# Sums of squares of the second attention's queries: four accumulating squares on ScalarE in place of one square and a VectorE reduction

## The chip, the cores and the metric

The kernel runs on one core of one Trainium2 chip. Its time is the device time of one execution in microseconds (us). A core has TensorE (PE in the rows: matrix products and transposes), VectorE (DVE), ScalarE (ACT), GpSimd (POOL) and SyncE (SP, which here issues DMAs). Each engine works through its own list of instructions in order, and they wait for one another by semaphores.

## What is computed

A transformer block in fp32 on 16 sequences of 128 tokens with 256 features: a first attention with adaptive layer norm (16 heads of 128), a GELU network, a second attention with 16 query heads and 4 key/value heads, and a mixture of 8 experts of which each token uses 2. The change lies in the second attention, where queries and keys are normalised head by head before the rotation:

```python
h = rmsnorm(hidden, attn_norm_w)
q = (h @ q_w.T).reshape(B, S, Hq, hd)        # Hq = 16, hd = 128
k = (h @ k_w.T).reshape(B, S, Hkv, hd)       # Hkv = 4
v = (h @ v_w.T).reshape(B, S, Hkv, hd)
q = rmsnorm(q, q_norm_w).transpose(0, 2, 1, 3)   # x * rsqrt(mean(x*x) + eps) * w
k = rmsnorm(k, k_norm_w).transpose(0, 2, 1, 3)
q = apply_rope(q, cos, sin)
k = apply_rope(k, cos, sin)
scores = jnp.einsum('bhqd,bhkd->bhqk', q, k) * scale   # causal, then softmax
attn = jnp.einsum('bhqk,bhkd->bhqd', jax.nn.softmax(scores, axis=-1), v)
hidden = hidden + attn @ o_w.T
```

The norm of a query head is a single factor for each token and head, so the kernel does not apply it to the query but to the scores: it is the scale of the exponential.

## The kernel before

Everything is written out in Bass: a list of instructions for each engine, with hand-placed semaphores. The products are made in three parts (high by high, high by low, low by high part of fp32 numbers split into two), so most results in PSUM are copied twice: ScalarE writes the high part, VectorE subtracts it and writes the low part.

The second attention runs from about 650 to 1100 us of the span. It is a software pipeline over 64 **units**: 16 sequences by 4 key/value heads (`kv`), a unit being the 4 query heads of one key/value head for the 128 tokens of one sequence, a tile of 128 x 512. `NG` = 4 groups of `GB` = 4 sequences, so 16 steps (`s.u` = 0 to 15) a group. `step(s)` on each engine does one stage for several units at once, and there are 7 more steps at the end in which no new unit is begun. In the step in which unit n is begun:

- **TensorE**: in the first step of each sequence the key projection into bank 1 and the value projection into bank 2; the query projection of unit n into bank 0 (L1958, 12 products with the split parts); the output product of unit n-6 (L2015); the product of weights and values of unit n-5 into bank 6 (L2042); transposes of the queries of unit n-1 into bank 4 (L2074) and of the weights of unit n-4 into bank 5 (L2082); mask and scores of unit n-2 into bank 3 (L2104, L2107). The next query projection waits for `g_qb` (rotation done) and `g_sq` (square done), since both read bank 0. The scores wait for `g_ex`, the exponentials of unit n-3 out of the same bank 3.
- **ScalarE**: the exponentials of unit n-3 (L891), four instructions of 128 x 128 with the scale `rq`, the bias `nb` and an accumulator that leaves the row sums in `rsum`; at a new sequence the square of the keys (L900); the square `sq` of the queries of unit n (L905, 128 x 512, out of bank 0); then the copies `o2_hi` (L912), `q_t` (L917), `pt_hi` (L924), and `v_hi` or `k_t` in the first or second step of a sequence.
- **VectorE**: the row maximum `nmax` of unit n-3 (L1552) and `nb` = `nmax` times `rq` (L1556); the rotation of keys (new sequence) and of queries out of banks 1 and 0, two instructions each (L1510, L1514); the reciprocal `rinv` of the row sums (L1578); the sum of squares of the keys; the sum of squares of the queries `q_ms` (L1589, a reduction of 128 x 512 to 128 x 4); then `o2_lo` (L1593), the residual `xres` once a sequence (L1598), `pt_lo` (L1601), `v_lo` once a sequence. Parts of norm, routing and weight splitting stand behind that, before the next step's `nmax`.
- **GpSimd**: adds the two parts of the rotation (L644), multiplies the weights by `rinv` (L648), and makes `rq` from `q_ms`: adds eps (L656), then the power -1/2 (L660). `rq` of unit n is used three steps later, by `nb` and by the exponentials. Once a sequence it does the same for the keys (`rk`).

`bank[6][:]` and the like are banks of PSUM, 512 fp32 numbers a partition each. The tile `p2` is called `p` in the rows of the trace and `p_123` in the lists of instructions; `o2_hi` and `o2_lo` are `o_hi` and `o_lo` there. The first attention (to about 560 us) and the experts (from about 1100 us) are not touched.

Of the kernel before, what the change touches and what calls it, by code (L numbers as in the profile page):

```python
# [23 lines left out]
ALU = mybir.AluOpType  # L24
ACT = mybir.ActivationFunctionType
X = mybir.AxisListType.X
# [4 lines left out]
GB = 4  # L31
NG = B // GB
GT = GB * T
H, DH = 16, 128
HKV = 4
REP = H // HKV
# [12 lines left out]
SCALE = DH ** -0.5  # L49
# [4 lines left out]
def program(nc, ins, out):  # L54
    ctx = ExitStack()
    with ctx:
# [15 lines left out]
        def sem(name):  # L72
            return ctx.enter_context(nc.semaphore(name))
# [75 lines left out]
        sq = sb("sq", [P, REP * DH], at=W2 + 6 * KB)  # L149
        kr = sb("kr", [P, HKV * DH], at=W2 + 8 * KB)  # L150
        kb = sb("kb", [P, HKV * DH], at=W2 + 10 * KB)
# [16 lines left out]
        q_ms = sb("q_ms", [P, 2, REP], at=small)  # L168
# [5 lines left out]
        nb = sb("nb", [P, 2, REP], at=small + 224)  # L174
# [63 lines left out]
        bank = [ctx.enter_context(nc.psum_tensor(f"bank{i}", [P, 512], F32)) for i in range(8)]  # L238
# [27 lines left out]
        def lo1(c, i):  # L266
# [24 lines left out]
            sem(f"g_{x}") for x in ("kp", "vp", "qp", "tp", "qtp", "op", "pvp", "ktp", "sp"))  # L291
        g_ex, g_ksq, g_sq, g_ph, g_vh, g_qt, g_oh, g_kt = (
            sem(f"g_{x}") for x in ("ex", "ksq", "sq", "ph", "vh", "qt", "oh", "kt"))
        g_x, g_mx, g_nb, g_kb, g_qb, g_ks, g_kr, g_pl, g_ss, g_ri, g_vl, g_ol = (
            sem(f"g_{x}") for x in ("x", "mx", "nb", "kb", "qb", "ks", "kr", "pl", "ss", "ri", "vl", "ol"))
        g_ka, g_rk, g_kv, g_qr, g_rq, g_qv, g_pn = (
            sem(f"g_{x}") for x in ("ka", "rk", "kv", "qr", "rq", "qv", "pn"))

# [87 lines left out]
        def _(sp):  # L386
# [73 lines left out]
            def load_tile(i):  # L460

                if i == 0:
                    sp.wait_ge(g_qr, NG * 4 * GB)
                    sp.wait_ge(g_ss, NG * 4 * GB)
                    sp.wait_ge(g_ktp, B)
                    sp.wait_ge(s_v, S_LIST)
                    sp.wait_ge(d_send[0], 16 * 2 * BC[0])
                if i == TC[0]:
                    sp.wait_ge(d_send[1], 16 * 2 * BC[1])
                if i >= NX:  # L470
                    sp.wait_ge(e_xp, i - NX + 1)
                    sp.wait_ge(s_goal, i - NX + 1)
                if i < TC[0]:
                    at = sp.value_load(base_i[0:1, i:i + 1], min_val=0, max_val=ROWS[0] - P)
                    sp.dma_start(xs[:, i % NX], xs_dram[0][bass.ds(at, P)]).then_inc(d_ring[i % NX], 16)
                else:
                    at = (i - TC[0]) * P
                    sp.dma_start(xs[:, i % NX], xs_dram[1][at:at + P]).then_inc(d_ring[i % NX], 16)
# [26 lines left out]
            for i in range(NX - 1):  # L505
                load_tile(i)
# [21 lines left out]
        def _(pool):  # L528
# [108 lines left out]
            def step(s):  # L637
                n, new_seq = s.n, s.new() and s.kv == 0
# [11 lines left out]
                                            ALU.mult).then_inc(g_pn, 1)  # L650
                if s.new():

                    pool.wait_ge(g_ss, n + 1)
                    if s.had(2):
                        pool.wait_ge(g_rq, n - 1)
                    nc.gpsimd.tensor_tensor(q_ve[:, s.u % 2], q_ms[:, s.u % 2], eps[:, 0:REP], ALU.add).then_inc(g_qv, 1)  # L656
                    pool.wait_ge(g_qv, n + 1)
                    if s.had(4):
                        pool.wait_ge(g_ex, n - 3)
                    nc.gpsimd.tensor_tensor(rq[:, s.u % 4], q_ve[:, s.u % 2], neg_half[:, 0:REP], ALU.pow).then_inc(g_rq, 1)  # L660
# [58 lines left out]
        def _(act):  # L719
# [105 lines left out]
            n = NG * H  # L825
# [47 lines left out]
            def step(s):  # L873
                n, new_seq = s.n, s.new() and s.kv == 0
# [10 lines left out]
                if s.live(3):  # L885
# [4 lines left out]
                    for j in range(REP):  # L890
                        last = nc.scalar.activation(p2[:, (s.u - 3) % 2, j], bank[3][:, j * T:(j + 1) * T], ACT.Exp,  # L891
                                                    scale=rq[:, (s.u - 3) % 4, j:j + 1],
                                                    bias=nb[:, (s.u - 3) % 2, j:j + 1],
                                                    accum_out=rsum[:, (s.u - 3) % 2, j:j + 1])
# [5 lines left out]
                    nc.scalar.activation(ksq[:], bank[1][:], ACT.Square, scale=SCALE).then_inc(g_ksq, 1)  # L900
                if s.new():
                    act.wait_ge(g_qb, n + 1)
                    if s.had(1):
                        act.wait_ge(g_ss, n)
                    nc.scalar.activation(sq[:], bank[0][:], ACT.Square, scale=SCALE).then_inc(g_sq, 1)  # L905
                if s.u == 12 and not s.first:
                    router_exp(s.g - 1)
                if s.live(5):
# [71 lines left out]
            def expert(i):  # L980
# [6 lines left out]
                if 0 <= i - 3 < NT:  # L987
                    expert_out(i - 3)

            attention2(step, expert)  # L990
            for i in range(len(DRAIN), NT + 3):
                expert(i)
# [7 lines left out]
        def _(dve):  # L1000
# [424 lines left out]
            n = NG * H  # L1425
# [93 lines left out]
            def step(s):  # L1519
                n, new_seq, prev = s.n, s.new() and s.kv == 0, 3 * NG + s.g - 1  # L1520
# [60 lines left out]
                if new_seq:  # L1581
                    dve.wait_ge(g_ksq, s.seq + 1)
                    nc.vector.tensor_reduce(k_ms[:], ksq[:].rearrange("p (h d) -> p h d", d=DH), X,
                                            ALU.add).then_inc(g_ks, 1)
                if s.new():
                    dve.wait_ge(g_sq, n + 1)
                    if s.had(2):
                        dve.wait_ge(g_rq, n - 1)
                    nc.vector.tensor_reduce(q_ms[:, s.u % 2], sq[:].rearrange("p (h d) -> p h d", d=DH), X,  # L1589
                                            ALU.add).then_inc(g_ss, 1)  # L1590
                if s.live(5):
                    dve.wait_ge(g_oh, n - 4)
                    nc.vector.tensor_tensor(o2_lo[:], bank[6][:], o2_hi[:].bitcast(F32), ALU.subtract).then_inc(g_ol, 1)  # L1593
# [674 lines left out]
```

## Time and profile before

| what | us |
|---|---|
| median of 3 runs | 1257.84 |
| lowest and highest of them | 1256.36, 1258.54 |
| the profiled execution | 1245.22 |
| its span (first to last instruction) | 1243.5 |
| VectorE busy | 793.6 (64%) |
| ScalarE busy | 655.5 (53%) |
| TensorE (matmul) busy | 1154.7 (93%) |
| GpSimd busy | 520.4 (42%) |

The profile is of one execution, which was 12.6 us shorter than the median of the runs. In the rows below, a time at the start of a row is the start of an instruction from the start of the span, and the bracket at its end is the idle time of that engine before it with what ended it. "PEld" is the weight load of TensorE, which overlaps its products.

### The profile page before, as it was taken

The page shows a single profiled execution, that of the slowest core. Times are in us where ns is not written, and L with a number is a line of the kernel's source. Part 1 is how long each engine was busy: PE and PEld are TensorE (multiplying, and loading weights), DVE is VectorE, ACT ScalarE, POOL GpSimd, SP SyncE. Part 2 cuts the span into 40 slices and gives each one's busy share as a digit, 9 for nine tenths or more (in the row PEclk, how much of TensorE's full clock was granted, in tenths as well). Part 3 has the DMA queues.
Part 4 walks back from the last instruction along what each step waited for, and adds up shares of the span by engine and source line. Part 5 has one row for each costly group of instructions (what it writes and reads, how often), then busy time and mean ns, then how long its engine had stood idle before and what let it go on. Part 6 is the DMA issues. An engine that isn't in the chain of part 4 may idle for free.

```text
span 1243.5 us, 23075 instructions
## 1 busy us (share of the span) xinstructions
PE 1154.7 (93%) x7776; PEld 1040.7 (84%) x7808; DVE 793.6 (64%) x1699; ACT 655.5 (53%) x1866; POOL 520.4 (42%) x597
## 2 busy tenths in 40 slices
PE   6999999999999999989988999998999999758995
PEld 5888999999999999978876888987887898657895
DVE  3666554345434553367557888888787888757666
ACT  3445444444444444465545766656756665545553
POOL 4111131113111311143347656665875786633753
PEclk9999999999999999999999999999999999989998
DMA  9100000000000011041001029400000100223546
GB/s 339 59 1 1 18 1 18 1 1 1 18 1 1 1 38 48 1 186 35 18 18 52 1 78 302 125 2 1 23 14 1 56 23 5 47 71 106 172 130 199
DMA packets 46454, 68.81 MB, mean 55 GB/s; under 512 B 4741, under 2 KB 38537, under 8 KB 45355
## 3 DMA queue, kind: packets, MB, share of 16 engines
q1 hardware_dynamic: 42595, 58.89, 15.2%
q0 software_dynamic: 3744, 8.43, 1.9%
q8 instruction: 66, 1.08, 0.4%
q14 instruction: 49, 0.40, 0.1%
HBM read 41.17 MB, written 27.97 MB: 56 GB/s over the span
## 4 chain that ended last, share of the span: by engine, by line
PE 67%; DVE 9%; ACT 6%; issue 4%; POOL 3%; DMA 2%; SPq 0%; ACTq 0%; DVEq 0%; POOLq 0%
PE bank L1770 12%; PE bank L1807 9%; PE bank L1958 7%; PE bank L1838 6%; PE bank L2015 5%; PE bank L1798 4%; PE bank L1780 4%; PE bank L2148 4%; PE bank L2107 3%; PE bank L2179 2%; ACT p L891 2%; PE bank L2042 2%; PE bank L1899 2%; PE bank L1788 2%; PE bank L2074 1%
## 5 line engine op out<-in xcount | busy, mean ns | idle before, releaser
L570 POOL TENSOR_TENSOR p<-p,rinv 128x512 f32<-128x512 f32 x64 | 66.5, 1040 | 409.3 <-DVE rinv L1340 409.3
L891 ACT ACTIVATE p<-bank,nb,rq 128x128 f32<-128x128 f32 x256 | 113.9, 454 | 133.4 <-DVE nb L1556 133.3
L760 ACT ACTIVATE p<-bank,nmax 128x128 f32<-128x128 f32 x256 | 90.7, 367 | 117.1 <-DVE nmax L1328 117.1
L644 POOL TENSOR_TENSOR qr<-qr,rb 128x512 f32<-128x512 f32 x64 | 81.6, 1276 | 95.7 <-DVE rb L1514 95.1
L1336 DVE COPY pt<-bank 128x512 f32<-128x512 f32 x64 | 44.2, 691 | 107.2 <-PE bank L1788 104.4
L1770 PE MATMUL bank<-cur_hi,wqk_hi 128*128 128x512 f32 x256 | 108.6, 424 | 4.1 <-DVE cur_lo L1281 4.1
L1770 PE MATMUL bank<-cur_hi,wqk_lo 128*128 128x512 f32 x256 | 101.5, 397 | 0.0
L1770 PE MATMUL bank<-cur_lo,wqk_hi 128*128 128x512 f32 x256 | 101.4, 396 | 0.0
L769 ACT ACTIVATE o_hi<-bank,bqkv 128x512 fp32r<-128x512 f32 x64 | 44.2, 691 | 100.3 <-PE bank L1798 100.0
L1344 DVE SCALAR_TENSOR_TENSOR o_lo<-bank,bqkv,o_hi 128x512 fp32r<-128x512 f32 x64 | 48.0, 751 | 52.8 <-ACT o_hi L769 52.8
L2107 PE MATMUL bank<-k_t,q_t 128*128 128x128 f32 x512 | 68.3, 277 | 12.3 <-ACT p L891 10.5
L1807 PE MATMUL bank<-wo_hi,o_hi 128*128 128x256 f32 x256 | 77.5, 303 | 0.6 <-DVE o_lo L1344 0.4
L2015 PE MATMUL bank<-wo_hi,o_hi 128*128 128x256 f32 x256 | 74.1, 289 | 4.2 <-DVE o_lo L1593 4.2
L1798 PEld LDWEIGHTS bank<-pt,v 128*128 128x128 f32 x512 | 66.3, 191 | 13.0 <-DVE pt L1336 8.5
L1838 PE MATMUL bank<-wv_hi,cur_hi 128*128 128x256 f32 x256 | 76.7, 300 | 0.0
L1798 PE MATMUL bank<-pt,v 128*128 128x128 f32 x512 | 67.9, 275 | 6.2 <-DVE pt L1336 6.2
L2015 PE MATMUL bank<-wo_hi,o_lo 128*128 128x256 f32 x256 | 72.9, 285 | 0.0
L2015 PE MATMUL bank<-wo_lo,o_hi 128*128 128x256 f32 x256 | 72.8, 285 | 0.0
L1807 PE MATMUL bank<-wo_hi,o_lo 128*128 128x256 f32 x256 | 72.2, 282 | 0.0
L1807 PE MATMUL bank<-wo_lo,o_hi 128*128 128x256 f32 x256 | 72.0, 281 | 0.0
L1838 PE MATMUL bank<-wv_lo,cur_hi 128*128 128x256 f32 x256 | 71.3, 278 | 0.0
L1838 PE MATMUL bank<-wv_hi,cur_lo 128*128 128x256 f32 x256 | 71.1, 278 | 0.0
(271 smaller groups left out, 3880.5 us busy)
## 6 DMA issues: line engine op xcount, KB each, us to landing
token_scratch<-empty SPq DMA_DIRECT2D x1, 13287.0 KB, 47.3
xs<-token_scratch SPq DMA_DIRECT2D x46, 129.0 KB, 2.2
wqk_raw<-in_wqk SPq DMA_DIRECT2D x8, 512.0 KB, 10.6
gate<-gates_scratch SPq DMA_DIRECT2D x8, 512.0 KB, 3.9
got_t<-expert_scratch SPq DMA_DIRECT2D x16, 256.0 KB, 3.7
w_raw<-in_w SPq DMA_DIRECT2D x2, 1408.0 KB, 6.3
xres<-in_x SPq DMA_DIRECT2D x4, 512.0 KB, 9.5
wv_raw<-in_wv SPq DMA_DIRECT2D x8, 256.0 KB, 10.5
```

What stands on the lines that cost most here:

```text
L570: nc.gpsimd.tensor_tensor(p1[:, h % 2], p1[:, h % 2], rinv[:, h % 2].unsqueeze(2).broadcast_to([P, GB, T]), ALU.mult).then_inc(a_pn, 1)
L644: nc.gpsimd.tensor_tensor(qr[:, s.u % 2], qr[:, s.u % 2], rb[:], ALU.add).then_inc(g_qr, 1)
L760: last = nc.scalar.activation(p1[:, h % 2, b], bank[3][:, b * T:(b + 1) * T], ACT.Exp, bias=nmax[:, h % 2, b:b + 1], accum_out=rsum[:, h % ...
L891: last = nc.scalar.activation(p2[:, (s.u - 3) % 2, j], bank[3][:, j * T:(j + 1) * T], ACT.Exp, scale=rq[:, (s.u - 3) % 4, j:j + 1], bias=n ...
L1770: last = pe.matmul(dst, l, r, start=(k == 0 and i == 0), stop=(k == KD - 1 and i == 2))
L1780: last = pe.matmul(bank[3][:, bs], q1[:, h % 2, bs], k1[:, h % 2, bs], start=True, stop=True)
L1798: last = pe.matmul(bank[5][:, bs], v1[:, h // 2 % 2, b, h % 2 * DH:h % 2 * DH + DH], pt1[:, bs], start=True, stop=True)
L1807: last = pe.matmul(bank[banks[b // 2]][:, b % 2 * D:b % 2 * D + D], l, r, start=(first and b % 2 == 0 and i == 0), stop=(last_one and i == 2),
L1838: last = pe.matmul(bank[2][:, j * 2 * DH:(j + 1) * 2 * DH], l, r, start=(k == 0 and i == 0), stop=(k == KD - 1 and i == 2))
L1958: last = pe.matmul(dst, l, r, start=(k == 0 and i == 0), stop=(k == KD - 1 and i == 2))
L2015: last = pe.matmul(bank[7][:, 0:D], l, r, start=(kv == 0 and j == 0 and i == 0), stop=(kv == HKV - 1 and j == REP - 1 and i == 2))
L2107: last = pe.matmul(bank[3][:, js], q_t[:, s.u % 2, js], k_t[:, slot, kv * T:(kv + 1) * T], start=False, stop=(j == REP - 1), skip_group_ch ...
```

## The change

ScalarE squares the queries in four instructions of 128 x 128, one for each head, and each leaves the sum of its row in `q_ms` by its accumulator. VectorE's reduction, its waits and its semaphore `g_ss` are gone; whoever waited for `g_ss` (GpSimd's L656, and SyncE once at the start of the experts) waits for `g_sq`. ScalarE no longer waits for the reduction of the unit before; it waits instead for `rq` of the unit two before, since it now writes `q_ms`. The squares themselves are still written to `sq`, which nobody reads.

```diff
@@ SyncE, before the first expert tile
-                    sp.wait_ge(g_ss, NG * 4 * GB)
+                    sp.wait_ge(g_sq, NG * 4 * GB)
@@ GpSimd, step
-                    pool.wait_ge(g_ss, n + 1)
+                    pool.wait_ge(g_sq, n + 1)
@@ ScalarE, step
                     act.wait_ge(g_qb, n + 1)
-                    if s.had(1):
-                        act.wait_ge(g_ss, n)
-                    nc.scalar.activation(sq[:], bank[0][:], ACT.Square, scale=SCALE).then_inc(g_sq, 1)
+                    if s.had(2):
+                        act.wait_ge(g_rq, n - 1)
+                    for j in range(REP):
+                        last = nc.scalar.activation(sq[:, j * DH:(j + 1) * DH], bank[0][:, j * DH:(j + 1) * DH], ACT.Square,
+                                                    scale=SCALE, accum_out=q_ms[:, s.u % 2, j:j + 1])
+                    last.then_inc(g_sq, 1)
@@ VectorE, step
-                if s.new():
-                    dve.wait_ge(g_sq, n + 1)
-                    if s.had(2):
-                        dve.wait_ge(g_rq, n - 1)
-                    nc.vector.tensor_reduce(q_ms[:, s.u % 2], sq[:].rearrange("p (h d) -> p h d", d=DH), X,
-                                            ALU.add).then_inc(g_ss, 1)
```

ScalarE in a plain step of the second group, with the semaphores that each instruction waits for. Before:

```order
L891 ACTIVATE p_123,rsum<-bank,nb,rq 128x128 [waits g_tp,g_nb]
L891 ACTIVATE p_123,rsum<-bank,nb,rq 128x128 x3
L905 ACTIVATE sq<-bank 128x512 [waits g_ss,g_qb]
L912 ACTIVATE o_hi<-bank 128x512 [waits g_op,g_pvp]
L917 ACTIVATE q_t<-bank 128x512 [waits g_sp,g_qtp]
L924 ACTIVATE pt_hi<-bank 128x512 [waits g_pvp,g_tp]
```

ScalarE at the same place, now:

```order
L891 ACTIVATE p_123,rsum<-bank,nb,rq 128x128 [waits g_tp,g_nb]
L891 ACTIVATE p_123,rsum<-bank,nb,rq 128x128 x3
L906 ACTIVATE sq,q_ms<-bank 128x128 [waits g_rq,g_qb]
L906 ACTIVATE sq,q_ms<-bank 128x128 x3
L915 ACTIVATE o_hi<-bank 128x512 [waits g_op,g_pvp]
L920 ACTIVATE q_t<-bank 128x512 [waits g_sp,g_qtp]
L927 ACTIVATE pt_hi<-bank 128x512 [waits g_pvp,g_tp]
```

The square has become four instructions at the same place, ahead of all three copies. The read-out that follows each accumulating instruction is not listed here; the trace shows it as ACTIVATION_READ_ACCUMULATOR.

## Rows read from the trace of the kernel before

**Rows 1.** The page, busy time of each engine, share of span, instructions:

```profile
PE 1154.7 (93%) x7776; PEld 1040.7 (84%) x7808; DVE 793.6 (64%) x1699; ACT 655.5 (53%) x1866; POOL 520.4 (42%) x597
```

**Rows 2.** Stretches: start:end, length, busy us per engine, granted clock, DMA:

```profile
774.17:799.44 25.27, 25.17 (x168) 22.77 (x169) 21.25 (x47) 17.03 (x51) 15.93 (x20) 1.00 0.65 184
700.00:1070.00 370.00, 355.25 (x2330) 314.77 (x2357) 305.30 (x647) 240.88 (x714) 251.74 (x306) 1.00 0.18 53
```

**Rows 3.** Waits from 700 to 1070 us: total us, times, longest:

```profile
ACT p L891 <- DVE nb L1556: 109.4, 54, 3.1
...
DVE pt_lo L1601 <- ACT pt_hi L924: 14.4, 41, 1.6
...
DVE q_ms L1589 <- ACT sq L905: 14.1, 41, 0.6
ACT o_hi L912 <- PE bank L2042: 7.0, 6, 1.2
...
ACT q_t L917 <- PE bank L2074: 4.4, 4, 1.2
...
DVE kr L1510 <- PE bank L1958: 2.7, 3, 0.9
```

**Rows 4.** Timeline of ScalarE in a plain step: start, duration, instruction:

```profile
789.91 0.46 ACT L891 ACTIVATE p<-bank,nb,rq 128x128 f32<-128x128 f32 x1 [1.19 <-DVE nb L1556]
...
791.24 0.46 ACT L891 ACTIVATE p<-bank,nb,rq 128x128 f32<-128x128 f32 x1
...
791.67 0.60 ACT L905 ACTIVATE sq<-bank 128x512 f32<-128x512 f32 x1
792.15 0.61 ACT L912 ACTIVATE o_hi<-bank 128x512 fp32r<-128x512 f32 x1
792.63 0.62 ACT L917 ACTIVATE q_t<-bank 128x512 f32<-128x512 f32 x1
793.11 0.63 ACT L924 ACTIVATE pt_hi<-bank 128x512 fp32r<-128x512 f32 x1
795.36 0.46 ACT L891 ACTIVATE p<-bank,nb,rq 128x128 f32<-128x128 f32 x1 [1.62 <-DVE nb L1556]
```

**Rows 5.** Timeline of VectorE in the same step:

```profile
792.31 0.69 DVE L1589 TENSOR_REDUCE q_ms<-sq 128x4 f32<-128x512 f32 x1 [0.31 <-ACT sq L905]
...
793.77 0.69 DVE L1601 TENSOR_TENSOR pt_lo<-bank,pt_hi 128x512 fp32r<-128x512 f32 x1 [0.18 <-ACT pt_hi L924]
794.37 0.68 DVE L1552 TENSOR_REDUCE nmax<-bank 128x4 f32<-128x512 f32 x1
795.16 0.16 DVE L1556 TENSOR_TENSOR nb<-nmax,rq 128x4 f32<-128x4 f32 x1
```

**Rows 6.** ScalarE in the first attention: two starts, then groups by form:

```profile
300.34 0.36 ACT L760 ACTIVATE p<-bank,nmax 128x128 f32<-128x128 f32 x1
...
300.68 0.37 ACT L760 ACTIVATE p<-bank,nmax 128x128 f32<-128x128 f32 x1
...
L760 ACT ACTIVATION_READ_ACCUMULATOR p<-bank,nmax 128x1 f32 x6 | 1.2, 200 | 0.0
...
L785 ACT ACTIVATE q<-bank,bqkv 128x512 f32<-128x512 f32 x1 | 0.7, 687 | 0.2 <-PE bank L1770 0.2
```

**Rows 7.** Timeline, second group: where ScalarE and VectorE waited for TensorE:

```profile
780.54 0.60 ACT L912 ACTIVATE o_hi<-bank 128x512 fp32r<-128x512 f32 x1 [1.24 <-PE bank L2042]
...
805.80 0.60 ACT L912 ACTIVATE o_hi<-bank 128x512 fp32r<-128x512 f32 x1 [1.09 <-PE bank L2042]
...
834.87 0.60 ACT L917 ACTIVATE q_t<-bank 128x512 f32<-128x512 f32 x1 [1.23 <-PE bank L2074]
...
860.51 0.69 DVE L1510 TENSOR_TENSOR kr<-bank,rope 128x512 f32<-128x512 f32 x1 [0.86 <-PE bank L1958]
```

**Rows 8.** Timeline, ScalarE's last read-out, then TensorE's scores after it:

```profile
772.49 0.21 ACT L891 ACTIVATION_READ_ACCUMULATOR p<-bank,nb,rq 128x1 f32 x1
...
772.90 0.38 PE L2104 MATMUL bank<-mask,ident_b 128*128 128x512 bf16 x1
...
848.55 1.05 PE L2107 MATMUL bank<-k_t,q_t 128*128 128x128 f32 x8 [1.36 <-ACT p L891]
```

More of the change, by code:

```diff
@@ L293, in program @@
             sem(f"g_{x}") for x in ("ex", "ksq", "sq", "ph", "vh", "qt", "oh", "kt"))
-        g_x, g_mx, g_nb, g_kb, g_qb, g_ks, g_kr, g_pl, g_ss, g_ri, g_vl, g_ol = (
-            sem(f"g_{x}") for x in ("x", "mx", "nb", "kb", "qb", "ks", "kr", "pl", "ss", "ri", "vl", "ol"))
+        g_x, g_mx, g_nb, g_kb, g_qb, g_ks, g_kr, g_pl, g_ri, g_vl, g_ol = (
+            sem(f"g_{x}") for x in ("x", "mx", "nb", "kb", "qb", "ks", "kr", "pl", "ri", "vl", "ol"))
         g_ka, g_rk, g_kv, g_qr, g_rq, g_qv, g_pn = (
```

## The prediction

> **What bounds the kernel now.** I read the page's busy times first, then the stretches, the waits and the timelines of the second attention, since the change touches nothing else. TensorE is busy for 93% of the span [rows 1] and for 355 of the 370 us from 700 to 1070 us [rows 2]; in a quiet sequence (774.17 to 799.44, four steps) it is busy for 25.17 of 25.27 us. That looks like a stretch bound by TensorE, behind which ScalarE (241 us busy of 370) could hide anything. The waits say that there is more to it. ScalarE waits for `nb` in all 54 steps, 109.4 us in all, about 2 us a step [rows 3], and this is no free time: it is the other half of a loop that runs through ScalarE and VectorE in every step. In a plain step the loop can be read off start by start [rows 4, 5]: first exponential 789.91 to square 791.67 (1.76), to `o_hi` 792.15 (0.48), to `q_t` 792.63 (0.48), to `pt_hi` 793.11 (0.48), to VectorE's `pt_lo` 793.77, which waited for `pt_hi` (0.66), to `nmax` 794.37 (0.60), to `nb` 795.16 (0.79), to the next exponential 795.36 (0.20). The sum is 5.45 us, which is the whole step. `nmax` stands behind `pt_lo` on VectorE, and the exponentials stand ahead of the copies on ScalarE, so no part of this loop can slip past another. TensorE's work for a plain step is as long, and in the first step of a sequence longer by the key and value projections. So two bounds lie side by side: TensorE is the later one at one or two points of each sequence, the loop in the steps between.
>
> How much room the loop has is what it waits for TensorE: `o_hi` 7.0 us in 6 waits, `q_t` 4.4 us in 4, `kr` 2.7 us in 3, together 14.1 us [rows 3]. In the second group these are 1.24 and 1.09 (`o_hi`, steps 4 and 8), 1.23 (`q_t`, step 12) and 0.86 (`kr`, step 0 of the next group) [rows 7].
>
> **What the change removes.** 64 reductions on VectorE, 0.69 us each and 0.60 from start to start [rows 5], 38 us. None of it is on the loop: in the plain step `pt_lo` still had to wait 0.18 us for `pt_hi` after reduction and `o_lo` were over [rows 5], and in 41 of 54 steps it did so, 14.4 us in all [rows 3]. Without the reduction `o_lo` can't begin earlier than `o_hi` ends, and `o_hi` now stands behind four squares. I cost the removal at 0. What hides it is ScalarE's chain of copies; were that chain shorter by more than 0.2 us a step, the reduction would be worth something.
>
> **What it adds.** On ScalarE one square, 0.48 us from its start to the start of `o_hi` [rows 4], becomes four of 128 x 128, each with a read-out of the accumulator. No row shows a square in this form. The nearest are the exponentials of the same shape with read-out: with scale and bias from memory 0.44 from start to start (789.91 to 791.24 is three of them, 1.33 us [rows 4]), with the bias alone from memory 0.34 (300.34 to 300.68 [rows 6]). Each operand from memory so costs about 0.09 us. The square has neither: at 128 x 512 it takes 0.60 [rows 4], while the copy with one such operand takes 0.687 [rows 6], the same 0.09. So I take 0.44 - 2 x 0.09 = 0.26 us for each square with its read-out, 1.04 for four, in place of 0.48: **d = 0.56 us a step**. The bounds: 0.20 each, if only the read-out itself (200 ns [rows 6]) is the limit, d = 0.32; 0.34 each, if an accumulating square costs what the cheaper exponential does, d = 0.90; 0.44 each, d = 1.28. The nearest is the middle of the first two, since both differences of 0.09 point there.
>
> The Trainium skill, page "ScalarE: Activation LUTs", section "What ACT_TABLE_LOAD costs", gives 186 ns plus 0.833 ns an element for an ACTIVATE with immediate operands, about 93 ns for each operand by pointer, and an overlap of about 93 ns between neighbours. The 0.09 of the rows agrees with its 93 ns; for the new square it gives 293 ns, and with a read-out of 200 ns and two overlaps 0.31 a square, d = 0.76, by which the steps below would come to +35 us.
>
> **Where d goes.** Squares stand beside exponentials in 61 of the 64 steps (the first three units come before the first exponential). If nothing took it up, the loop would be 61 x 0.56 = 34 us longer. I go from one wait on TensorE to the next; there the loop's delay is taken up as far as TensorE was late, but TensorE itself has meanwhile been pushed by the exponentials, behind which its scores stand. In the second group:
> - Steps 1 to 4, to the `o_hi` that waited 1.24. TensorE's scores follow ScalarE's last read-out at 772.49 + 0.21 within 0.2 us, and all after it ran without a break [rows 8]. It is pushed by the squares of steps 0, 1 and 2, 3d less under 0.1, 1.6 us; the loop by 5d - 1.24 = 1.6. The later counts: +1.6.
> - Steps 5 to 8, `o_hi` waited 1.09: 4d - 1.09 = +1.15. TensorE arrived later than the exponentials here and is pushed less.
> - Steps 9 to 12, `q_t` waited 1.23: 4d - 1.23 = +1.0.
> - Steps 13 to 16. The routing on VectorE makes the loop longer and TensorE waits for it, 1.36 us at once at 848.55 [rows 8]. So it is pushed in full by three squares: 3d - 0.15 = +1.5; the fourth is taken up by the 0.86 of `kr`.
>
> That is 5.3 us for the second group and as much for the third; in the last nothing takes up the fourth square, 5.4. The first group has no wait for TensorE but a `q_t` of 0.7 (4.4 less three of 1.23 [rows 3]) and the next group's `kr` (0.9): 15 x 0.56 less 0.7 and 0.7 = 7.0. Sum 23 us, less about 1 for waits too short for the list: **+22 us**. After the last square the pipeline drains into the experts as before, and carries the delay to the end.
>
> **Other edits.** GpSimd waits for `g_sq` in place of `g_ss`. The last read-out ends about 3 x 0.26 + 0.4 = 1.15 us after the first square's start; the reduction ended at 792.31 + 0.69 = 793.00, 1.33 after 791.67. `rq` comes 0.2 us earlier, and is used three steps later: 0. TensorE's next query projection waits for `g_sq`, which now comes 0.5 us later; in a plain step it is still in its scores by then, cost 0 to 0.3 us once a group. The new wait of ScalarE for `rq` of two units before has been met a step ago; queued behind it are the squares and all copies, but it costs 0. SyncE's wait falls after the last unit, 0.
>
> **Rivals.**
> - *Hidden.* TensorE, at 96% in this stretch, sets the pace and ScalarE's 2 us a step of idle time take the 0.56. For it speaks that in the quiet sequence TensorE never waits; against it, that the loop fills the plain step to the last 0.01. It would give 0 to +2 us, 1258.
> - *Dear read-outs.* The square costs 0.34 with its read-out. By the same steps with d = 0.90: 12.1 for the first group, then 10.7, 10.7 and 10.8, +44 us, 1302. At 0.44 it is +68.
> - *VectorE relieved, faster.* In 13 of 54 steps `pt_lo` did not wait for `pt_hi` [rows 3]; there VectorE may be the late one, and the loop would run `sq`, `q_ms`, `o_lo`, `pt_lo`. Without `q_ms` 13 x 0.6 = 8 us come off, 1250. It decides from d under 0.2, where the four squares end no later than reduction and `o_lo` let the loop go; the bound of 0.20 a square already gives d = 0.32.
> - *Nothing taken up*, +34 us, 1292: the waits on TensorE go along with the loop. I count it to the upper half of the forecast.
>
> **How the numbers follow.** The profiled execution took 1245.2 us, with a span of 1243.5; it is 12.6 under the median of the runs, 1257.8, and I put the 22 us on the median: 1280. Chances: forecast and its margins (+6 to +36) 0.71, dear read-outs (+36 to +70) 0.11, hidden or almost (within 2.5 us, 0.2%, about what a measurement of this kernel can tell) 0.10, a small loss of 2.5 to 6 us 0.02, faster 0.06. So slower 0.84, same 0.10, faster 0.06. The range, 1264 to 1302, runs from d = 0.32 (by the same steps +0.9, +0.2, +0.1 and +0.8 in a group, some 10 us with the first, and a little below) to d = 0.90, and leaves out the hidden case, the gain and the dearest read-outs, 0.2.
>
> **What would show it.** In the profile after: squares 0.28 us long, 0.26 from start to start; a plain step of 6.0 us from exponential to exponential; waits of `o_hi` and `q_t` for TensorE nearly gone; TensorE idle before the scores (waiting for exponentials) in most steps, up by some 20 us; `pt_lo` waiting about 0.7 us for `pt_hi` in each step; VectorE busy 38 us less, ScalarE some 36 us more. The forecast is wrong if the squares start 0.34 or more apart, or if the plain step stays at 5.45 us.

## The result, and the profile after

The changed kernel takes **1282.03 us** (median of 4 runs, 1277.19 to 1283.62), the kernel before beside it 1257.87 (1256.36 to 1258.54). That is 24.2 us more, a ratio of **1.0193, 95% interval 1.0164 to 1.0221**. The forecast was 1280, range 1264 to 1302, slower with a chance of 0.84.

The profiled execution of after took 1281.76 us, with a span of 1280.0, 36.5 more than the span of before. Only some 26 of these belong to the change, as the windows show (start:end, length, busy us of TensorE, weight load, VectorE, ScalarE and GpSimd, then granted clock, DMA). First after, from the first exponential to the last and from there to the end:

```profile
667.10:1123.10 456.00, 413.20 (x2622) 360.71 (x2652) 319.09 (x695) 310.96 (x1252) 293.14 (x346) 0.98 0.16 48
1123.10:1280.00 156.90, 126.89 (x811) 113.97 (x810) 93.03 (x278) 71.20 (x204) 70.28 (x66) 0.89 0.43 131
```

Before, the same two stretches:

```profile
664.50:1096.70 432.20, 401.77 (x2626) 355.44 (x2656) 354.73 (x756) 278.12 (x825) 291.92 (x347) 1.00 0.17 50
1096.70:1243.50 146.80, 118.09 (x809) 106.80 (x807) 96.38 (x278) 70.58 (x204) 70.14 (x66) 0.92 0.46 140
```

The pipeline grew by 23.8 us and began 2.6 later. The experts' part behind it, which the change doesn't touch, was 10.1 longer, with a granted clock of 0.89 where it was 0.92. In a second profile of the same kernel (e5 below) it lasted 146.9 us, as before, and between 144.7 and 148.5 in those of e1, e2, e3, e6, e7, e8 and e9. So these 10 us are no effect of the change.

The busy times answer [rows 1]. VectorE has 42 us less, ScalarE 35 more:

```profile
PE 1177.2 (92%) x7776; PEld 1055.7 (82%) x7808; DVE 751.2 (59%) x1635; ACT 690.8 (54%) x2314; POOL 524.0 (41%) x597
```

The squares and their read-outs, all of them: least, median and greatest duration in ns, first and last start.

```profile
L906 ACT ACTIVATE sq<-bank x256: 268/281/308, 652.8 to 1101.3; 128x128 f32<-128x128 f32 x128
L906 ACT ACTIVATION_READ_ACCUMULATOR sq<-bank x256: 194/215/243, 652.9 to 1101.5; 128x1 f32 x128
```

ScalarE in a plain step, against [rows 4]. Line numbers are 3 higher than before from the squares' code down to the removed reduction, and 3 lower behind it; the names are the same:

```profile
800.90 0.46 ACT L891 ACTIVATE p<-bank,nb,rq 128x128 f32<-128x128 f32 x1 [1.14 <-DVE nb L1559]
...
802.66 0.28 ACT L906 ACTIVATE sq<-bank 128x128 f32<-128x128 f32 x1
802.82 0.21 ACT L906 ACTIVATION_READ_ACCUMULATOR sq<-bank 128x1 f32 x1
802.91 0.29 ACT L906 ACTIVATE sq<-bank 128x128 f32<-128x128 f32 x1
...
803.66 0.64 ACT L915 ACTIVATE o_hi<-bank 128x512 fp32r<-128x512 f32 x1
804.14 0.64 ACT L920 ACTIVATE q_t<-bank 128x512 f32<-128x512 f32 x1
804.62 0.65 ACT L927 ACTIVATE pt_hi<-bank 128x512 fp32r<-128x512 f32 x1
806.89 0.46 ACT L891 ACTIVATE p<-bank,nb,rq 128x128 f32<-128x128 f32 x1 [1.62 <-DVE nb L1559]
```

VectorE in the same step, against [rows 5]:

```profile
804.33 0.69 DVE L1590 TENSOR_TENSOR o_lo<-bank,o_hi 128x512 fp32r<-128x512 f32 x1 [1.34 <-ACT o_hi L915]
805.30 0.69 DVE L1598 TENSOR_TENSOR pt_lo<-bank,pt_hi 128x512 fp32r<-128x512 f32 x1 [0.28 <-ACT pt_hi L927]
805.91 0.68 DVE L1555 TENSOR_REDUCE nmax<-bank 128x4 f32<-128x512 f32 x1
806.69 0.16 DVE L1559 TENSOR_TENSOR nb<-nmax,rq 128x4 f32<-128x4 f32 x1
```

The loop, start by start: exponential to square 1.76, four squares to `o_hi` 1.00 (one square had 0.48), `q_t` 0.48, `pt_hi` 0.48, `pt_lo` 0.68, `nmax` 0.61, `nb` 0.78, next exponential 0.20. The sum is 5.99 us against 5.45, and all but 0.02 of the difference is the squares. VectorE has no reduction any more, and stands idle for 1.34 us until `o_hi` comes.

The waits from 700 to 1100 us, against [rows 3] (total us, times, longest):

```profile
ACT p L891 <- DVE nb L1559: 114.1, 56, 3.4
...
DVE o_lo L1590 <- ACT o_hi L915: 72.5, 55, 1.6
...
DVE pt_lo L1598 <- ACT pt_hi L927: 17.1, 42, 1.4
...
PE bank L2104 <- ACT p L891: 12.9, 11, 2.3
PE bank L2101 <- ACT p L891: 9.0, 13, 2.1
...
ACT q_t L920 <- PE bank L2071: 3.5, 4, 1.0
...
PE bank L1955 <- ACT sq L906: 0.2, 1, 0.2
```

The idle time that VectorE won turned into a new wait of its own, for `o_hi`, 72.5 us in 55 steps. The wait of `o_hi` for TensorE, 7.0 us in [rows 3], is gone; that of `q_t` is only down from 4.4 to 3.5. TensorE's query projection (L1955) waited for the squares only once here, 0.2 us.

Where the delay builds up, read from the start of an exponential at each boundary (us; "e5" is the second profile of the same kernel):

| exponential | before | after | e5 | added, after | added, e5 | forecast |
|---|---|---|---|---|---|---|
| the first | 664.46 | 667.10 | 666.28 | 2.6 | 1.8 | 0 |
| second group | 751.21 | 760.83 | 758.67 | 7.0 | 5.6 | 7.0 |
| third group | 859.70 | 874.22 | 871.93 | 4.9 | 4.8 | 5.3 |
| fourth group | 968.96 | 989.05 | 988.12 | 5.6 | 6.9 | 5.3 |
| the last | 1096.72 | 1123.10 | 1123.38 | 6.3 | 7.5 | 5.4 |

Each row gives what was added since the row above it. Step by step, from first exponential to first exponential, 10 of the 16 steps of the second group (counted from 0) grew by 0.49 to 0.55 us, step 0 by 0.42 and step 9 by 0.67. Step 1 stayed as it was. Steps 4, 8 and 12, in which `o_hi` or `q_t` had waited for TensorE, became shorter by 0.62, 0.65 and 0.24. So the squares cost their 0.52 in steps of every length, not in the plain ones alone, and are taken up above all where TensorE had been late.

### The profile page after: what moved, and what is told of

It reads as the page before. It is cut to its first block, busy times and chain, and to the rows that moved or that the text cites. A ratio compares the mean times of both kernels' runs of the same rounds, so it can differ in the third digit from the quotient of the medians.

```text
span 1280.0 us, 23396 instructions
## 1 busy us (share of the span) xinstructions
PE 1177.2 (92%) x7776; PEld 1055.7 (82%) x7808; DVE 751.2 (59%) x1635; ACT 690.8 (54%) x2314; POOL 524.0 (41%) x597
## 3 DMA queue, kind: packets, MB, share of 16 engines
q1 hardware_dynamic: 42595, 58.89, 14.6%
## 4 chain that ended last, share of the span: by engine, by line
PE 53%; DVE 13%; ACT 12%; issue 6%; POOL 5%; DMA 2%; another core or an unknown queue 0%; SPq 0%; ACTq 0%; DVEq 0%; POOLq 0%
PE bank L1767 11%; PE bank L1804 9%; PE bank L1835 6%; ACT p L891 4%; PE bank L1795 4%; PE bank L2145 4%; PE bank L1955 4%; PE bank L1777 4%; ACT sq L906 3%; PE bank L2176 2%; DVE nmax L1555 2%; DVE pt_lo L1598 2%; PE bank L1785 2%; PE bank L1896 2%; PE bank L2012 2%
## 5 line engine op out<-in xcount | busy, mean ns | idle before, releaser
L1590 DVE TENSOR_TENSOR o_lo<-bank,o_hi 128x512 fp32r<-128x512 f32 x64 | 44.3, 692 | 82.5 <-ACT o_hi L915 82.5
L2104 PE MATMUL bank<-k_t,q_t 128*128 128x128 f32 x512 | 69.7, 280 | 17.2 <-ACT p L891 16.2
L906 ACT ACTIVATE sq<-bank 128x128 f32<-128x128 f32 x256 | 67.5, 284 | 15.7 <-DVE rb L1517 14.8
```

The costliest lines, as they stand in the source:

```text
L906: last = nc.scalar.activation(sq[:, j * DH:(j + 1) * DH], bank[0][:, j * DH:(j + 1) * DH], ACT.Square, scale=SCALE, accum_out=q_ms[:, s.u ...
L2104: last = pe.matmul(bank[3][:, js], q_t[:, s.u % 2, js], k_t[:, slot, kv * T:(kv + 1) * T], start=False, stop=(j == REP - 1), skip_group_ch ...
```

## The experiments

My theory is the prediction's: a loop through ScalarE and VectorE binds the plain steps, the squares lie on it and the reduction didn't, and TensorE's lateness in the first step of a sequence takes a little back. The rivals are that something else carries the cost (TensorE's projection behind `g_sq`, the read-outs alone) and that the reduction was worth something after all. Differences in us are of medians, ratios come from the paired comparison; the two can differ by up to 1.7 us. The chips of these runs were some 11 us faster for both kernels than that of the first result: the kernel before took 1246.4 in the runs of e1 to e4, 1246.6 in those of e5 to e8, and 1244.6 in those of e9 to e11. The whole times in the expectations of e1 to e4 were worked out from the first result, so only their differences can be held against what was measured.

**e5, the changed kernel again**, unedited, for its difference on these chips.

> The changed kernel again, beside the others of this call. +22 to +26 us against the kernel before on the same chip, whatever that chip's level is; the pipeline of the second attention longer by 24 to 27 us, the experts and the first attention the same but for TensorE's granted clock.

Measured: 1271.1, +24.5 us, ratio 1.0205 [1.0181, 1.0229]; plain step 5.98. The level of the chip doesn't change the difference. Against this number the others are read.

**e2, the reduction away and the square left whole.** GpSimd adds eps to the first four squares of the tile, in place of the sums, so the normalisation of the queries is left out.

```diff
-                    nc.gpsimd.tensor_tensor(q_ve[:, s.u % 2], q_ms[:, s.u % 2], eps[:, 0:REP], ALU.add).then_inc(g_qv, 1)
+                    nc.gpsimd.tensor_tensor(q_ve[:, s.u % 2], sq[:, 0:REP], eps[:, 0:REP], ALU.add).then_inc(g_qv, 1)
...
-                    for j in range(REP):
...
+                    if s.had(1):
+                        act.wait_ge(g_qv, n)
+                    nc.scalar.activation(sq[:], bank[0][:], ACT.Square, scale=SCALE).then_inc(g_sq, 1)
```

> Only the removal: one square of 128x512 as before and no reduction on VectorE; GpSimd makes rq from four of the squares (so the query norm is not the reference's). The loop theory: the reduction was beside the loop, 0 to -3 us against the kernel before (1255 to 1258). Rival, that VectorE was the late one in the steps where pt_lo did not wait: -8 us or more, below 1250.

Measured: 1246.77 against 1246.4, ratio 0.9993 [0.9980, 1.0006]; plain step 5.44. The removal by itself, 64 reductions and 38 us of VectorE's time, is worth nothing. The rival by which a relieved VectorE gains 8 us falls.

**e7, the split alone**: in the kernel before, four plain squares without an accumulator, reduction kept.

```diff
-                    nc.scalar.activation(sq[:], bank[0][:], ACT.Square, scale=SCALE).then_inc(g_sq, 1)
+                    for j in range(REP):
+                        last = nc.scalar.activation(sq[:, j * DH:(j + 1) * DH], bank[0][:, j * DH:(j + 1) * DH], ACT.Square,
+                                                    scale=SCALE)
+                    last.then_inc(g_sq, 1)
```

> The kernel before with four squares of 128x128 without accumulator, and the reduction kept. Start to start 0.28 - 0.12 = 0.16 us, four of them 0.65 in place of 0.48: d = 0.17. Between two reads of the waits on TensorE: +2 to +6 us. Rival, the number of ScalarE instructions is what costs, not the read-out: above +12.

Measured: 1253.04, +6.5 us, ratio 1.006 [1.0038, 1.0081], plain step 5.63. Timeline of ScalarE in e7; the four squares stand in one row:

```profile
790.48 0.79 ACT L906 ACTIVATE sq<-bank 128x128 f32<-128x128 f32 x4
791.13 0.63 ACT L915 ACTIVATE o_hi<-bank 128x512 fp32r<-128x512 f32 x1
```

Four squares take 0.65 us to the start of `o_hi`, 0.16 each, in place of 0.48. With its read-out each takes 0.25. So of the 0.52 us a step 0.17 is the split and 0.35 the four read-outs, and of the 24.5 us about 6.5 and 18, the split counted first. In this profile TensorE's granted clock fell to half twice (862 to 866 and 975 to 978 us), so part of the 6.5 us may be the clock's; the plain step isn't touched by it.

**e3, two squares of 128 x 256 with accumulator.** Two sums a row stand in for four, so the queries of two heads share one.

```diff
-                    for j in range(REP):
-                        last = nc.scalar.activation(sq[:, j * DH:(j + 1) * DH], bank[0][:, j * DH:(j + 1) * DH], ACT.Square,
+                    for j in range(2):
+                        last = nc.scalar.activation(sq[:, j * 256:(j + 1) * 256], bank[0][:, j * 256:(j + 1) * 256], ACT.Square,
```

> The changed kernel with two accumulating squares of 128x256 in place of four of 128x128 (each sum is over two heads, so the norm is not the reference's). Start to start 0.25 + 128 x 0.83 ns = 0.36 us, two of them 0.71 in place of 0.48: d = 0.23 us a step. With the waits on TensorE taking up delay as predicted: 2.1 in the first group, then about 1.2 each, +6 us (1263). Rival, each microsecond on ScalarE counts in proportion (24 us for 0.55): +10 us (1268). Rival, the read-out as such is dear: above 1270.

Measured: 1254.79, +8.4 us, ratio 1.0062 [1.0040, 1.0084], plain step 5.69. Timeline of ScalarE in e3:

```profile
801.11 0.38 ACT L908 ACTIVATE sq<-bank 128x256 f32<-128x256 f32 x1 [0.76 <-DVE rb L1519]
...
801.49 0.38 ACT L908 ACTIVATE sq<-bank 128x256 f32<-128x256 f32 x1
...
801.84 0.60 ACT L917 ACTIVATE o_hi<-bank 128x512 fp32r<-128x512 f32 x1
```

Two squares take 0.73, +0.25 a step, half of what four add, for about a third of the time.

**e6, eight squares of 128 x 64**, the odd ones with their sums into a spare tile; each of the four sums that are used is then over half a head.

```diff
-                    for j in range(REP):
-                        last = nc.scalar.activation(sq[:, j * DH:(j + 1) * DH], bank[0][:, j * DH:(j + 1) * DH], ACT.Square,
-                                                    scale=SCALE, accum_out=q_ms[:, s.u % 2, j:j + 1])
+                    for j in range(2 * REP):
+                        last = nc.scalar.activation(sq[:, j * 64:(j + 1) * 64], bank[0][:, j * 64:(j + 1) * 64], ACT.Square,
+                                                    scale=SCALE, accum_out=(q_ms, q_hx)[j % 2][:, s.u % 2, j // 2:j // 2 + 1])
```

> The changed kernel with eight accumulating squares of 128x64 (each sum is over half a head, so the norm is not the reference's). Start to start 0.25 - 64 x 0.83 ns = 0.20 us, eight of them 1.58 in place of 0.48: d = 1.1 us a step. Now the waits on TensorE are used up: by the steps of the prediction 15 in the first group, then 14 each, +57 us. Rival, in proportion to the 24 us of d = 0.55: +48. Rival, ScalarE's idle 2 us a step still take it (TensorE or the clock set the time): within 35.

Measured: 1305.69, +59.1 us, ratio 1.0481 [1.0457, 1.0505]; plain step 6.60. Timeline of ScalarE in e6, the first two squares and `o_hi`:

```profile
821.83 0.22 ACT L907 ACTIVATE sq<-bank 128x64 f32<-128x64 f32 x1 [0.77 <-DVE rb L1518]
...
822.04 0.22 ACT L907 ACTIVATE sq<-bank 128x64 f32<-128x64 f32 x1
...
823.42 0.65 ACT L916 ACTIVATE o_hi<-bank 128x512 fp32r<-128x512 f32 x1
```

Eight squares take 1.59 us, d = 1.11. Added squares pass on to the end almost whole once the waits that can take them up are used up: 0.59 more a step made 34.6 us more, where 61 steps of it are 36. TensorE's query projection now waited for the squares too, 17.5 us in 33 waits over the whole stage (3.4 in 5 in the changed kernel), but the plain step is still the loop: 5.99 with the squares' 1.00 replaced by 1.59 is 6.58.

Together, d = 0, 0.17, 0.25, 0.52 and 1.11 gave 0, +6.5, +8.4, +24.5 and +59.1 us. This is no straight line through zero: of the first quarter of a microsecond about half is hidden, of the rest little.

**e1, the changed kernel with `pt_hi` ahead of `q_t`.** It takes one copy of 0.48 us off the loop and leaves ScalarE's work the same.

```diff
-                if s.live(1):
-                    act.wait_ge(g_qtp, n)
...
                 (pt_hi)
+                if s.live(1):
+                    act.wait_ge(g_qtp, n)
...
```

> The changed kernel, with ScalarE's copies q_t and pt_hi in the other order in each step (pt_hi first). The loop theory (exponentials, squares, o_hi, q_t, pt_hi, then VectorE's pt_lo and nmax, set the step): q_t leaves the loop, 0.48 us a step, so the plain step falls from 6.0 us to TensorE's 5.5, and the kernel loses nearly all of the 24 us: 1260, between 1256 and 1266. Rival, that TensorE is held by the later end of the squares (it reads bank 0 only after them) or by anything else than this loop: no change, 1278 to 1284, plain step 6.0 us.

Measured: 1261.48, +15.1 us against the kernel before, ratio 1.0109 [1.0092, 1.0125]. 9.4 of the 24.5 us came back, not nearly all. Timeline of VectorE in e1, a plain step:

```profile
804.40 0.69 DVE L1590 TENSOR_TENSOR o_lo<-bank,o_hi 128x512 fp32r<-128x512 f32 x1 [1.34 <-ACT o_hi L915]
805.00 0.68 DVE L1598 TENSOR_TENSOR pt_lo<-bank,pt_hi 128x512 fp32r<-128x512 f32 x1
805.60 0.68 DVE L1555 TENSOR_REDUCE nmax<-bank 128x4 f32<-128x512 f32 x1
```

`pt_lo` no longer waits for anything: it stands behind `o_lo`, which begins 0.67 us after `o_hi` and takes 0.60. The loop now runs squares, `o_hi`, `o_lo`, `pt_lo`; it is 5.60 us long and not 5.5, still 0.15 over the kernel before. That the loop binds is shown, since an exchange of two copies of equal work is worth 9 us. The squares lie on both of its branches. The measured 1261.48 lies in the expected 1256 to 1266 only because this chip is faster; by the difference, +15 where about +2 was expected, the expectation failed. The rival, no change at all, falls as well. 61 steps of 0.15 are 9 of the 15.1 us; the rest lies in the first units and in the steps that are not plain, and I didn't take it apart.

**e4, the same exchange in the kernel before** (the diff is that of e1, with its square whole and its reduction kept).

> The kernel before with the same swap as e1, pt_hi ahead of q_t. Loop theory: the loop is 0.48 us shorter in each step, but TensorE's 5.5 us bound the plain step already, so only the steps in which TensorE waited for exponentials gain: -4 to -12 us (1246 to 1254). Rival, TensorE or VectorE alone bounds it: no change.

Measured: 1246.79 against 1246.4, ratio 0.9999 [0.9981, 1.0018]. The plain steps did become shorter, 5.45 to 5.17, with VectorE's reduction now on the loop (timeline of VectorE in e4: three instructions without a gap, the first after the square):

```profile
819.12 0.69 DVE L1589 TENSOR_REDUCE q_ms<-sq 128x4 f32<-128x512 f32 x1 [0.31 <-ACT sq L905]
819.72 0.68 DVE L1593 TENSOR_TENSOR o_lo<-bank,o_hi 128x512 fp32r<-128x512 f32 x1
820.32 0.68 DVE L1601 TENSOR_TENSOR pt_lo<-bank,pt_hi 128x512 fp32r<-128x512 f32 x1
```

But the first step of a sequence gave it all back: 8.48 us in place of 7.91 (801.09 to 809.57), with `o_hi` waiting for TensorE, then `pt_hi` too. Timeline of ScalarE there:

```profile
805.49 0.60 ACT L912 ACTIVATE o_hi<-bank 128x512 fp32r<-128x512 f32 x1 [1.37 <-PE bank L2042]
806.37 0.60 ACT L919 ACTIVATE pt_hi<-bank 128x512 fp32r<-128x512 f32 x1 [0.28 <-PE bank L2082]
```

**e11, e2 with the exchange**: no reduction and the shorter loop. The normalisation is left out as in e2, and its edit is those of e2 and e1 together.

> e4 (pt_hi ahead of q_t) and e2 (one square, no reduction; the query norm is not the reference's) together. In e4 the reduction is on the loop, so ScalarE and VectorE now need less than 5.17 us a plain step. If TensorE's work is the other bound throughout, as e4 says, nothing comes of it: -3 to +2 us against before. If the loop still held the kernel, -5 to -10.

Measured: 1242.72 against 1244.56, ratio 0.9991 [0.9971, 1.0011], plain step 5.07. Even 0.38 us less loop in each plain step is worth nothing measurable. Before, TensorE was the other bound, as close behind as the prediction had it: 25.17 of 25.27 us in a quiet sequence [rows 2]. The loop can be made longer at a price and not shorter at a gain.

**e8 and e9, the new form for the first unit of a sequence alone, and for the other three alone.** The rest keeps the whole square and the reduction.

```diff
+        ACC = (0,)
...
+                    if s.kv in ACC:
...
+                        for j in range(REP):
+                            last = nc.scalar.activation(sq[:, j * DH:(j + 1) * DH], bank[0][:, j * DH:(j + 1) * DH],
+                                                        ACT.Square, scale=SCALE, accum_out=q_ms[:, s.u % 2, j:j + 1])
+                        last.then_inc(g_sq, 1)
+                    else:
+                        nc.scalar.activation(sq[:], bank[0][:], ACT.Square, scale=SCALE).then_inc(g_sq, 1)
...
-                if s.new():
+                if s.new() and s.kv not in ACC:
```

In e9 it is `ACC = (1, 2, 3)`.

> The change in the first step of each sequence only (16 of 64 units; one square and the reduction in the other 48). If the waits on TensorE take up delay where they stand, d is taken up there whole: steps 4, 8 and 12 of a group cost nothing, step 0 some 0.5, together 0 to +3 us against before. Rival, each of the 64 costs its share of 24 us: +6 us.

> The complement of e8: the change in the second, third and fourth step of each sequence (48 of 64 units), one square and the reduction in the first. If the waits on TensorE in the first steps take up delay: the 24.5 us less the 2.1 of e8, and less again because three delays of 0.53 meet a wait of 1.1 to 1.2 instead of four: by the steps of the prediction about 3d - 1.2 or 2d a sequence, +12 to +19 us. Rival, each unit costs its share: +18.4.

Measured: e8 1248.64, +2.1 us, ratio 1.002 [1.0005, 1.0035]; e9 1267.66, +23.1, ratio 1.0193 [1.0142, 1.0244]. Timeline of ScalarE in e8, where [rows 7] had `o_hi` waiting 1.24 us:

```profile
781.00 0.29 ACT L919 ACTIVATE sq<-bank 128x128 f32<-128x128 f32 x1
...
781.72 0.60 ACT L930 ACTIVATE o_hi<-bank 128x512 fp32r<-128x512 f32 x1 [0.34 <-PE bank L2060]
```

The 16 first units cost 2 us where 16 times 0.52 would be 8.3, and most of the missing 6.2 us are such waits: from 700 to 1100 us those of `o_hi` fell from 7.0 to 3.4, those of `q_t` from 4.4 to 2.7. The other 48 cost 23.1 (17.7 to 30 by the interval; its pipeline, first exponential to last, 20.1), against 48 times 0.52 = 25: a fifth at most is taken up. The interval still reaches into the +12 to +19 that I expected. My +12 to +19 for e9 let TensorE's waits take up as much as they had been long. They took less, since TensorE, behind later exponentials, was itself later: in e9 `o_hi` still waited for it in 3 steps, up to 0.6 us, though the first step of the sequence had no added square. The two parts add to 25.2, the whole is 24.5.

**e10, the squares behind `pt_hi`**, off the loop and onto TensorE's next projection.

```diff
-                    for j in range(REP):
-                        last = nc.scalar.activation(sq[:, j * DH:(j + 1) * DH], bank[0][:, j * DH:(j + 1) * DH], ACT.Square,
...
                 (o_hi, q_t, pt_hi)
+                    for j in range(REP):
+                        last = nc.scalar.activation(sq[:, j * DH:(j + 1) * DH], bank[0][:, j * DH:(j + 1) * DH], ACT.Square,
...
```

> The changed kernel with the four squares behind pt_hi on ScalarE, in its wait for nb. They leave the loop (ScalarE and VectorE alone would need 4.97 us a plain step), but TensorE's next query projection waits for them: squares, projection, output product, weights times values, transposes, pt_hi, squares = 1.1 + 1.4 + 1.4 + 0.7 + 0.9 + 0.6 = 6.1 to 6.3 us a plain step. So it is no faster than the changed kernel: +20 to +40 us against before, with TensorE waiting for the squares about 0.6 us in each plain step. If only ScalarE's chain to pt_hi counted, it would come to before or below (-5 to +3).

Measured: 1276.28, +31.7 us, ratio 1.0268 [1.0215, 1.0321]. Waits in e10, 700 to 1100 us, and TensorE's timeline in one step:

```profile
ACT o_hi L907 <- PE bank L2039: 41.3, 31, 2.7
```

```profile
802.27 0.47 PE L1955 MATMUL bank<-wq_hi,cur_hi 128*128 128x512 f32 x1 [0.80 <-ACT sq L925]
```

TensorE waits for the squares (31.6 us in 41 steps of this stretch), and then ScalarE for TensorE, 41.3 us. Neither of the two places that were tried is free: ahead of the copies the squares lengthen one loop, behind them the other. Places between the copies were not tried.

## Why the prediction was right, and where it was off

The direction, the mechanism and the total hold. By its steps:

- **Removal, 0.** Shown by e2.
- **d = 0.56 a step.** Measured 0.52 in the loop, 0.25 a square where 0.26 was taken; the bounds of 0.20 and 0.34 were both further off. The estimate from the Trainium skill ("ScalarE: Activation LUTs", section "What ACT_TABLE_LOAD costs") had been 0.31. Its duration comes close, 293 ns against a median of 281. Its overlap of about 93 ns between neighbouring ACTIVATEs was 0.12 us between plain squares here (0.28 long, 0.16 apart, e7). For a read-out the page gives no overlap; the prediction took 93 ns there too, and this is what was off: square and read-out together last 281 + 215 = 496 ns and start 250 apart, an overlap of 246, where two of 93 are 186. The estimate of +35 us was about 11 too much.
- **The loop, 61 squares.** Shown: plain step 5.99 (forecast 6.0), and by e1. The first three units, which the prediction counted at nothing, are the term that was missed: the first exponential came 2.6 and 1.8 us later in the two profiles (next section).
- **The first group.** The prediction adds up 15 squares there. In the trace 13 stand between the first exponential and that of the second group, as its own 61 = 13 + 3 x 16 says, so its sum should have been 13 x 0.56 - 1.4 = 5.9 and not 7.0. Measured are 5.6 in e5, and 5.7 in after without the 1.3 us that half a clock cost there (next section). That 7.0 stands in the table for after is luck.
- **What TensorE takes up.** Right in kind (e8 and the shortened steps 4, 8, 12), wrong in its single sizes. In the second group the four segments came to 0.9, 0.9, 1.5 and 1.6 against 1.6, 1.15, 1.0 and 1.5. The forecast of the first leaves out a wait for GpSimd: in step 1 of this group, before, VectorE's `kr` (L1570) waited 0.61 us for `rk`, and ScalarE's square behind the rotation 0.63; after, both waits are gone and so is one square's cost. In the third group, where before has no such wait, the first segment came to 1.4. The third segment came out higher than forecast in both groups (1.5 and 1.65): step 9 grew by more than its squares (0.67 and 0.82), and step 12 became shorter by only 0.24. Why step 9 did is not shown. By groups, without what the clock added in three steps, 5.7, 4.9, 5.6, 6.3 in after and 5.6, 4.8, 5.4, 6.1 in e5 stand against 7.0 (5.9), 5.3, 5.3, 5.4.
- **The sum.** That +22 lies so near to +24.2 is in part luck. Without the clock's share the pipeline grew by 22.5 and 22.0 us in the two profiles. At the measured 0.52 the 61 squares are 31.7, so 9 to 10 were taken up, where the forecast took 12 off 34. The cost a square was put too high and what is taken up too high as well, and the missed first units weigh against the two squares too many.
- **Signs that failed.** I expected `pt_lo` to wait 0.7 us for `pt_hi` in each step. It waits 0.28, since `o_lo` stands ahead of it and took over the wait, 1.34 us. Had I seen that, I would have known what e1 can give back: `pt_lo` can come forward only to the end of `o_lo`, 0.28 us and the 0.09 by which neighbours overlap, 0.37 of the 0.48. TensorE's waits for exponentials rose from 12.0 (700 to 1070 us, before) to 21.9, by 10 us and not by 20. The wait of `q_t` did not nearly vanish.
- **Rivals.** Hidden, relieved and "dear read-outs" fall by e5, e2 and the 0.25. "Nothing taken up" (+34, or 31.7 at the measured 0.52) is excluded by e5's interval, 22.6 to 28.5 us. That TensorE's projection behind `g_sq` carries the cost falls by its 0.2 us of waiting from 700 to 1100 us; only in the first units does it wait for them (3.4 us in 5 waits over the whole stage).

My own expectations failed in e1, e4 and e9. Each time I shortened or lengthened one loop and let the other stand still. That of e7 was 0.5 us too low at its upper end (+6.5 against +2 to +6), and e3 came out between the forecast of +6 and the rival of +10.

## What the runs showed beside

**TensorE at half clock in the first units.** The third query projection of the stage, at 659.90, waits for the squares of the second unit. TensorE's timeline there, after:

```profile
659.90 0.77 PE L1955 MATMUL bank<-wq_hi,cur_hi 128*128 128x512 f32 x1 [1.23 <-ACT sq L906]
660.46 0.63 PE L1955 MATMUL bank<-wq_lo,cur_hi 128*128 128x512 f32 x1
660.88 0.63 PE L1955 MATMUL bank<-wq_hi,cur_lo 128*128 128x512 f32 x1
```

And before:

```profile
659.05 0.47 PE L1958 MATMUL bank<-wq_hi,cur_hi 128*128 128x512 f32 x1 [0.80 <-ACT sq L905]
659.36 0.39 PE L1958 MATMUL bank<-wq_lo,cur_hi 128*128 128x512 f32 x1
659.60 0.39 PE L1958 MATMUL bank<-wq_hi,cur_lo 128*128 128x512 f32 x1
```

After, the products start 0.43 us apart, before 0.23, at a granted clock of 0.50 (660 to 663) against 1.00: 1.2 against 2.4 GHz. From the projection's first product to the transposes it is 2.69 us and not 1.48. With 0.30 for the stage's own start, 0.55 for the squares ahead and 0.56 for those of the third unit, this makes the 2.6 us of the first exponential. In e5 the clock fell half way through this projection (2.06 us), and the first exponential was 1.8 late. Other runs bear the term out. From the stage's first rotation of keys (`kr`) to the first exponential it was 14.6 us before and 14.5, 15.0 and 15.0 in e2, e11 and e4, which keep the whole square; it was 16.8, 16.2, 16.5 and 16.9 in after, e5, e1 and e9.

**A wait doesn't fix the clock by itself.** Inside the pipeline, after 2.08 us of waiting for exponentials, the clock fell in one execution and not in the other. After:

```profile
727.38 0.38 PE L2101 MATMUL bank<-mask,ident_b 128*128 128x512 bf16 x1 [2.08 <-ACT p L891]
...
729.28 0.63 PE L1955 MATMUL bank<-wkv_lo,cur_hi 128*128 128x512 f32 x1
```

The same place in e5:

```profile
726.46 0.38 PE L2101 MATMUL bank<-mask,ident_b 128*128 128x512 bf16 x1 [2.06 <-ACT p L891]
...
727.80 0.39 PE L1955 MATMUL bank<-wkv_lo,cur_hi 128*128 128x512 f32 x1
```

The step with this stretch lasted 8.96 us in after and 7.68 in e5. e5 has two stretches of its own, ahead of the first steps of the third and of the last group. TensorE's timeline at the second of them, the output product, in e5:

```profile
985.00 0.58 PE L2012 MATMUL bank<-wo_hi,o_hi 128*128 128x256 f32 x1 [0.75 <-DVE o_lo L1590]
985.38 0.42 PE L2012 MATMUL bank<-wo_lo,o_hi 128*128 128x256 f32 x1
```

And in after:

```profile
985.92 0.39 PE L2012 MATMUL bank<-wo_hi,o_hi 128*128 128x256 f32 x1 [0.76 <-DVE o_lo L1590]
986.15 0.28 PE L2012 MATMUL bank<-wo_lo,o_hi 128*128 128x256 f32 x1
```

The wait ahead is the same, 0.75 us, but from 985 to 988 the granted clock is 0.50 in e5 and 1.00 in after, and the next products start 0.21 and not 0.12 us apart. The key projection ends later, `kr` waits 2.12 us for it and not 0.74, and the step lasts 10.82 us and not 9.45. At the head of the third group it is the same (0.50 from 869 to 872, a step of 10.95 and not 9.46). These three steps, 1.3, 1.5 and 1.4 us, are all by which the two profiles differ by more than 0.2 us in a row of the table behind the first. A stretch at half clock need not cost anything: that of after from 684 to 687 left its two steps at 6.86 and 6.43 us, where e5 has 6.85 and 6.42. Whether longer waits make such stretches more frequent stays open. Between 670 and 1060 us before has none and after and e5 have two each, but e2, where the squares add nothing, had one too (0.86 between 685 and 695 us), and e10, one of the slowest, none.

**ScalarE's pitch, start to start**: a square of 128 x 512 0.48 us; of 128 x 128 0.16 without and 0.25 with accumulator; 128 x 256 with it about 0.365, 128 x 64 0.20. An accumulator costs about 0.09 at 128 x 128, far less than the 0.21 that its read-out lasts, and the split costs as well.

## What to carry to other kernels

Before moving work to an engine that is idle half the time, add up the loop that crosses engines in one step, start to start: if the sum is the step, idle time on either engine is no room, and only the place of the work in the in-order streams counts. Taking work away pays only if nothing else ends within the same interval, so look at the wait of the next instruction behind it. Where two bounds lie side by side, a delay costs, at first in part (e3, e7) and then nearly whole (e6), and a gain pays nothing (e4, e11); that moving both would pay was not tried.
